# One step of the table split for each gather unit, raw tables loaded through the picks' staging memory, in a DLRM tower on one core

## The reference

```python
e = jnp.stack([tbl_f[ids[:, f]] for f in range(32)], axis=1)   # [2048, 32, 256]
dots = jnp.einsum('bnd,bmd->bnm', e, e)
z = dots[:, iu, ju]                                            # i < j: 496 values
h = jnp.concatenate([z, dense_ctx], axis=1)
h = jnp.maximum(h @ W_top1 + b_top1, 0.0)                      # 512
h = jnp.maximum(h @ W_top2 + b_top2, 0.0)                      # 256
y = h @ W_top3
```

## Time and profile before

| | us |
|---|---|
| median of 3 runs (lowest, highest) | 605.2 (604.75, 606.4) |
| profiled execution, its own time | 607.6 |
| its span | 605.8 |
| POOL busy in the span | 432.1 |
| PE busy in the span | 528.5 |
| DVE, ACT busy in the span | 277.2, 217.3 |

### The profile page before, as it was taken

How to read it: one execution, slowest core, us unless ns; L and a number is a source line. 1 busy time by engine, 2 the same in 40 slices (tenths; PEclk the granted TensorE clock), 3 DMA queues, 4 the chain that set the end, 5 groups by cost and what they waited for, 6 DMA issues and landing times.

```text
span 605.8 us, 24947 instructions
## 1 busy us (share of the span) xinstructions
PE 528.5 (87%) x11450; PEld 464.4 (77%) x11450; DVE 277.2 (46%) x604; ACT 217.3 (36%) x423; POOL 432.1 (71%) x463
## 2 busy tenths in 40 slices
PE   1458998999989898998899989998988898998997
PEld 0234795998979797887888788887968788796776
DVE  2002753827454555536354554626455461715143
ACT  1223234344333434333333433342343333333442
POOL 6776577777777777777777777777777777777720
PEclk9999999999999999999999999999999999998999
DMA  5588453343434343433434343343434333333310
GB/s 145 190 232 229 122 151 108 110 126 108 124 107 122 111 125 110 124 109 106 124 108 122 111 125 109 109 126 108 122 108 122 110 108 110 110 107 108 106 47 1
DMA packets 26411, 72.10 MB, mean 119 GB/s; under 512 B 8426, under 2 KB 9338, under 8 KB 25680
## 3 DMA queue, kind: packets, MB, share of 16 engines
q0 software_dynamic: 21888, 59.80, 35.1%
q1 hardware_dynamic: 4420, 10.72, 5.7%
HBM read 70.48 MB, written 0.01 MB: 116 GB/s over the span
## 4 chain that ended last, share of the span: by engine, by line
PE 65%; DMA 13%; POOL 12%; issue 7%; ACT 1%; DVE 1%; SPq 0%
PE ps_l L327 18%; PE ps_turn L243 15%; DMA rows<-in_table,index 13%; POOL rows L230 12%; PE ps_gram L294 12%; PE ps_pick L272 6%; PE ps_pick L274 6%; PE ps_l L341 2%; PE ps_l L258 1%; PE ps_l L361 1%; PE ps_pick L258 1%; PE ps_l L349 1%; DVE pairs L604 0%; PE ps_wide L281 0%; PE ps_gram L311 0%
## 5 line engine op out<-in xcount | busy, mean ns | idle before, releaser
L230 POOL DMA_INDIRECT rows<-in_table,index x456 | 431.3, 946 | 147.3 <-issue 116.4
L461 ACT COPY cols<-ps_turn 128x512 f32<-128x512 f32 x221 | 128.3, 589 | 324.1 <-PE ps_turn L243 323.6
L604 DVE COPY pairs<-ps_gram 32x112 f32<-32x112 f32 (+1 forms) x484 | 181.5, 375 | 128.6 <-PE ps_gram L294 122.4
L243 PE MATMUL ps_turn<-identity,rows 128*128 128x128 f32 x912 | 148.0, 291 | 53.1 <-DMA rows<-in_table,index 52.3
L243 PEld LDWEIGHTS ps_turn<-identity,rows 128*128 128x128 f32 x912 | 102.4, 145 | 74.0 <-DMA rows<-in_table,index 51.2
L294 PE MATMUL ps_gram<-cols 128*32 128x32 f32 x7936 | 109.6, 201 | 18.8 <-issue 17.2
L294 PEld LDWEIGHTS ps_gram<-cols 128*32 128x32 f32 x7936 | 90.0, 111 | 44.4 <-issue 39.7
L591 DVE TENSOR_TENSOR one_hot<-ps_wide,row_number 125x2048 fp32r<-125x2048 f32 x28 | 63.9, 2281 | 122.8 <-ACT ps_wide L478 102.5
L272 PE MATMUL ps_pick<-one_hot,table_hi 125*128 125x256 f32 x448 | 114.3, 293 | 0.4 <-ACT stage L482 0.4
L327 PE MATMUL ps_l<-pairs,w_sb 128*128 128x128 f32 x960 | 109.9, 276 | 0.7 <-DVE score L623 0.7
L274 PE MATMUL ps_pick<-one_hot,table_lo 125*128 125x256 f32 x448 | 109.6, 283 | 0.0
(11 more groups left out here) (68 smaller groups left out, 144.4 us busy)
## 6 DMA issues: line engine op xcount, KB each, us to landing
rows<-in_table,index POOLq DMA_INDIRECT x456
pick_id<-in_pick_ids SPq DMA_DIRECT2D x14, 250.0 KB
w_sb<-in_w_t SPq DMA_DIRECT2D x1, 2048.0 KB, 23.5
cols<-in_tbl SPq DMA_DIRECT2D x2, 1000.0 KB
stage<-in_tbl SPq DMA_DIRECT2D x2, 1000.0 KB
w_sb<-in_W_top SPq DMA_DIRECT2D x1, 512.0 KB, 26.7
pairs<-in_dense_t SPq DMA_DIRECT2D x16, 8.0 KB, 2.1
scores<-score SPq DMA_DIRECT2D x16, 0.5 KB
```

The lines of the kernel that those rows point to most:

```text
L230: pool.indirect_dma_start(out=rows[x % ROWS][:, k, :], out_offset=None, in_=table, in_offset=bass.IndirectOffsetOnAxis(ap=index[:, t, i:i ...
L243: last = pe.transpose(ps_turn[x % TURNS][:, h, SPG * k:SPG * (k + 1), :], rows[x % ROWS][:, k, h * P:(h + 1) * P], identity[:, :])
L461: act.copy(cols[t % COLS][:, :, :, FPU * u:FPU * (u + 1)], ps_turn[x % TURNS][:, :, :, :]).then_inc(cols_ready, 1)
L604: last = dve.tensor_copy(pairs[n % 2][N_FIELDS * q:N_FIELDS * (q + 1), c0:KC, per * j + s0:per * j + s0 + FQ] .rearrange("p c g -> p g c") ...
```

## The change

The split is spread out: `piece(t, u)` gives one piece to a unit. Pieces 0 to 3 (table 0) stand after T12 to T15, pieces 4 to 7 (table 1) after T16 to T19, pieces 8 to 11 (table 2) after T25 to T28, piece 12 after T31, and pieces 13 to 15 after T32 to T34. `split_table` becomes `split_piece`, `take_lo` moves from DVE to ACT, behind the evacuation of the same unit. Pieces 0 to 7 all use the PSUM area of layer 1, pieces 8 to 15 that of the picks, so each piece waits for the copy of the one before, and piece 8 for the second pick to be taken (`stage_ready` 2). `make_hi` stands ahead of the evacuation of units 11, 15, 24 and 30. Raw table 0 goes to `stage[0]`, and tables 1, 2 and 3 all to `stage[1]`, so table 2 is loaded when 8 pieces are done and table 3 when 12 are. The weights no longer wait for table 1 and have no table ahead of them. The loads of ids and dense inputs in the tile loop stand behind both table loads in SP's order.

```diff
+    def piece(t, u):
+        if t == 1 and u >= 4:
+            return u - 4
+        if t == 2 and u < 4:
+            return PIECES + u
+        if t == 3 and 1 <= u <= 4:
+            return 2 * PIECES + u - 1
+        if t == 3 and u == ALL - 1:
+            return 3 * PIECES
+        if t == BPG and u < 3:
+            return 3 * PIECES + 1 + u
+        return -1
...
-        table_raw = [flat[0:VP, :].rearrange("p (c d) -> p c d", c=VC) for flat in
-                     [cols[COLS - 1][:, h, :, :].rearrange("p s f -> p (s f)") for h in range(HALVES)] +
-                     [stage[1][:, :, :, :].rearrange("p h s j -> p (h s j)")] * 2]
+        table_raw = [stage[g][0:VP, :, :, :].rearrange("p h s j -> p (h s j)").rearrange("p (c d) -> p c d", c=VC)
+                     for g in (0, 1, 1, 1)]
...
             sp.wait_ge(table_loaded[0], 16)
-            load_table(2)
-            sp.wait_ge(table_loaded[1], 16)
             sp.dma_start(w1_sb[:, :, :], w1_t).then_inc(w1_loaded, 16)
...
-            sp.wait_ge(low_done, 3 * PIECES)
-            load_table(3)
+            for j in (2, 3):
+                sp.wait_ge(low_done, j * PIECES)
+                load_table(j)
...
-            def split_table(j):
-                pe.wait_ge(hi_ready, j + 1)
-                if j == 3:
-                    pe.wait_ge(hidden1_ready, 1)
+            def split_piece(x):
+                j, i = x // PIECES, x % PIECES
+                if i == 0:
+                    pe.wait_ge(hi_ready, j + 1)
+                if x >= 1:
+                    pe.wait_ge(lo_ready, x)
+                if x == 2 * PIECES:
                     pe.wait_ge(stage_ready, 2)
...
-                        pe.wait_ge(lo_ready, PIECES * (3 if j < 2 else 4))
+                        pe.wait_ge(lo_ready, PIECES * (4 if j >= 2 else j + 1))
...
                     if n == 0:
                         pe.wait_ge(w1_loaded, 16)
+                        pe.wait_ge(lo_ready, 2 * PIECES)
...
-                    pe.wait_ge(lo_ready, PIECES * PICKS)
...
-                    if t == 1 and u in (4, 5, 6):
-                        split_table(u - 4)
-                    if t == 3 and u == 6:
-                        split_table(3)
+                    if piece(t, u) >= 0:
+                        split_piece(piece(t, u))
...
+            def take_lo(x):
+                j, i = x // PIECES, x % PIECES
+                act.wait_ge(low_done, x + 1)
+                act.copy(table_lo[:, j, :, :].rearrange("p c d -> p (c d)")[:, 512 * i:512 * (i + 1)],
+                         ps_low[0 if x < 2 * PIECES else 1]).then_inc(lo_ready, 1)
...
-                    if t == 1 and u in (4, 5, 6):
-                        make_hi(u - 4)
-                    if t == 3 and u == 6:
-                        make_hi(3)
+                    if (t, u) in ((1, 3), (1, 7), (3, 0), (3, 6)):
+                        make_hi({(1, 3): 0, (1, 7): 1, (3, 0): 2, (3, 6): 3}[t, u])
                     evacuate(t, u)
+                    if piece(t, u) >= 0:
+                        take_lo(piece(t, u))
```

More of the change, by code:

```diff
@@ L253, in split_table @@
                 hi_v = table_hi[:, j, :, :].rearrange("p c d -> p (c d)")
[L254 to L261, removed]
+                low = ps_low[0 if x < 2 * PIECES else 1]
+                pe.matmul(low, identity[0:VP, 0:VP], raw_v[:, 512 * i:512 * (i + 1)], start=True, stop=False)
+                pe.matmul(low, minus_identity[0:VP, 0:VP], hi_v[:, 512 * i:512 * (i + 1)],
+                          start=False, stop=True).then_inc(low_done, 1)
             def pick(q, h):
@@ L650, in _ @@
             dve.wait_ge(numbers_ready, 1)
[L652 to L657, removed]
             make_one_hot(0)
@@ L666, in _ @@
             for t in range(1, BLOCKS):
[L667 to L670, removed]
                 if t % 2 == 1 and t < JOBS:
                     make_one_hot(t)
-                if t == 3:
-                    take_lo(3)
                 if t % 2 == 0 and 4 <= t < BLOCKS:
```

## The result

The changed kernel takes 623.4 us (median of 6 runs, 622.65 to 624.81) beside 605.3 for the kernel before (6 runs): a ratio of 1.029, 95% interval 1.0268 to 1.0313, so 18 us more. The forecast was 618.5 in a range of 608 to 625. The profiled execution of the changed kernel took 624.8, its span is 622.9.

The account below looks back on a forecast made before the run. POOL's 456 gathers of 1.25 us set the pace, so time follows POOL's summed stalls: from 6.6 to 16.9 lateness plus 3 clock, 19.9, is 13.3 us more, 605.2 + 13.3 = 618.5 us, range 608 to 625.

Parts of the forecast that it names:

- The scale: POOL's gathers: T of unit x must end by 23.46 + 2.5x; the greatest lateness equals POOL's summed stalls, 6.6 us before.
- Spreading: One piece after each of T12 to T19: piece 7 ends at 67.5 (66 to 69.5), POOL's three early stalls go.
- Copies on ACT: 16 copies of about 0.58 us move from DVE to ACT's free time: nothing, or at most 0.3 us for a few pieces.
- First wait: Table 2's load, 12.5 us, lands at 80.1; piece 8 starts at 83.8, PE idles 3.9 us.
- Second wait: Table 3's load, 12.5 us, lands at 110.9; PE idles about 10 us ahead of piece 12, T41's lateness is 16.9.
- Clock: PE runs partly at half rate after idling: 1 and 2 us for the two idle times, 3 together (0 to 6).
- Weights sooner at 0: Weights load 11.4 us earlier, same hole in the gathers on T7 to T10: no cost (0 to 2 us, gain up to 1.5).
- The cap of the gain (2.3 us): T41's lateness of 4.3 us stays, PE having no rest from T12 to T41, so gain is at most about 2.3.
- (B): Table loads take 7 to 10 us and only table 3 is waited for: 609.6 us (606 to 613), chance 0.10.
- (C): Table loads are hidden, only T41's lateness of 3 to 4.3 us remains: faster, 602 to 603 us, chance 0.08.
- L: Time of one late table load with its completion: taken as 12.5 us, bounds 7 and 13.5.
- (D): Weights' hole in the gathers is deeper as table 1 competes, and the clock costs 6: above 624 us, chance 0.06.

Follow-up runs that it names:

- copies_on_dve: The changed kernel with the 16 copies of the low parts back on DVE, in one particular order: 631.0 us, ratio 1.0410 to the kernel before.
- warm_waits: The changed kernel with 4 idle matmuls ahead of piece 8 and 11 ahead of piece 12, filling PE's waits: 622.4 us, ratio 1.0258 to before.
- before_fan: The kernel before with only each table loaded as two DMAs of 112 and 13 partitions: 603.25 us, ratio 0.9949.
- fan_loads: The changed kernel with every raw table loaded by two DMAs of 112 and 13 partitions: 604.95 us, ratio 0.9997 to the kernel before.
- early_paced_12: The changed kernel with spread loads, tables 2 and 3 in separate buffers, requested after pieces 3 and 7, table 3's pieces behind T31 to T34: 599.5 us.

## Why the prediction was right

The forecast growth was 13.3 us and the measured one 18.1. The profiled execution grew by 17.2: 16.1 of stalls and 1.1 of POOL's slower beat; the last 0.9 is that the profiled executions lie differently to their medians. So 2.8 us of the 4.8 missing are stalls, and they are placed below.

*The scale (T must end by 23.46 + 2.5x, S the greatest lateness): right.* T26 ended at 95.41, lateness 6.95, and the first stall is 6.85; T41 at 148.81, lateness 22.85, and the stalls sum to 22.7.

*Spreading: right.* Piece 7 was to end at 67.5 and ended at 67.8, no stall of POOL before 95. That this came within 0.3 us is luck, since errors cancel in it. The clock was full by piece 0, which saves about 2.5 us (pieces 0, 1 and 2 took 2.1, 2.1 and 1.5 us before, and 1.1 each is the full price); ACT's copies held PE 1.5 us; the rest is small differences of the matmuls behind them, and T12 ended hardly sooner (48.8 against 49.0).

*Copies on ACT: right in size (1.5 us, within the bound), wrong in the reason.* 1.07 of it is the copy behind the rounding of table 1, which the upper bound of piece 7 allowed for, and the two others are 0.23 each. But DVE did not have the time that its share suggested (copies_on_dve).

*First wait: right in place and length.* Piece 8 at 83.8 forecast, 83.88 measured; PE idle 3.9 and 3.78. Load 12.5 and 12.5.

*Second wait: right in place, the load 0.6 short.* Table 3 took 13.1. PE idled 11.6 where I had about 10: 0.6 by the load and 1.0 because it had 3.5 us of work left up to T31, not 4.5; this second error does not count, as the load sets the end.

*Clock: mechanism right, size too small.* I gave 1 us to the first idle time and 2 to the second. From piece 8 to T26 it took 11.5 us where I had 8.7, 2.8 more; from piece 12 to T32 3.35 where I had 1.7. warm_waits gives 2.6 and 1.5 back on PE. The first was the larger, since layer 1 stands right behind it: it took 8.83 us instead of 7.31, and piece 8 2.3 instead of 1.1. What I read at the start of the earlier trace rows was loose too: T13 stands behind 8.6 us of PE's unbroken work, not 5. Of the 2.8 us between the forecast growth of S (13.3) and the measured one (16.1) the clock makes 1.5 (4.5 for 3), the load of table 3 0.6, the stretch T32 to T41 0.4 (28.7 for 28.3) and that from T26 to the request of table 3 0.3 (6.3 for 6.0). The slower beat of POOL, 1.1 us, I can't place.

*Weights sooner at 0: wrong.* It costs 2.7 us in the kernel before. In the changed one it costs 2.3 at piece 7 and nothing in S; the ratio is 1.029 against 1.0238 without it, but that difference is one of beat and tail in the traces. The step failed where it said that the same hole falls with the same room. It did not change the forecast, since T12 in the changed kernel still started at the time that I had taken over from before.

*The cap of the gain (2.3 us): too low in general.* The forecast did not rest on it. before_fan keeps the old order and reaches S of 1.2, since PE starts T12 3.7 us earlier (44.2 for 47.9) and T41 ends 3.7 earlier. PE also had some rest between T12 and T41, against what I wrote: it waited 3.2 us in all, though none behind T32.

*Rivals.* (B) needed quicker loads; fan_loads made them, S was 5.8 where (B) had 11 at 8.5 us, and piece 7 came 9 us earlier. (C) is what early_paced_12 does, once the loads are early, spread and paced. Its condition was loose: L under 6.1 us only brings the time back to that of before, and its S of 3 to 4.3 needs L under 4 by the same sum. (D) came in part: the hole was deeper (0.35 for 0.41 MB) and the clock cost 4.5 us, but no gather stalled before 50 us, and the time stayed under 624, by 0.6 us.

## What to carry to other kernels

When several loads share a staging buffer, find for each load what releases it and what in an in-order queue wants it next; if less work than one load lies between, the engines that wait for that queue stop, and the price is paid again by each such load (6 and 9 us here). Before shortening an engine's work, find which engine's beat sets the end, turn the others' work into due times against it, and look at the second-latest due time: it limits the gain in that order. Large loads need a place in time and a shape that spreads, also when nothing waits for them, since the gathers do.

## What the runs showed that I had not expected

- Loads that nobody waits for were worth 3 us: spreading the tables in the kernel before lowers it from 606.6 to 603.25.
- The weights' load takes the gathers' share of the queues, 0.35 MB in 8.7 us, though POOL issues 0.91. It is 0.64 with no table in flight beside the weights, and they then land in 10.4 us instead of 22.7.
- A table load of an eighth of the bytes took 4.3 us, a third of the whole one's 12.5 to 13.1.
- Nearly equal waits of PE at the same place, 2.87 and 2.76 us, were followed by a half clock once and by the full clock the other time.
- The tail behind the last gather differed by up to 2.7 us between kernels that do the same work there (24.0 to 26.7), and by 5.6 with warm_waits. This is as much as some of the effects above, and what sets it is open.
